# Four indirect row scatters of a GpSimd slot, moved from its end into two pairs between the norm and modulation steps

## What is computed

```python
h = layernorm(x) * (1 + ca) + sa          # norm 1 and its modulation
h = ln(h, ln1_g, ln1_b)                   # norm 2
xm = mix(h, att_time_mix, att_combined_mix)
k, v, r = exp(min(xm @ Wk.T, 60)), xm @ Wv.T, xm @ Wr.T
h = h + sigmoid(r) * wkv(time_decay, time_first, k, v) @ Wo.T
h = ln(h, ln2_g, ln2_b)                   # norm 3
xm = mix(h, ffn_time_mix, ffn_combined_mix)
h = h + sigmoid(xm @ Fr.T) * (square(relu(xm @ Fk.T)) @ Fv.T)
x = x + ga * h
h = layernorm(x) * (1 + cb) + sb          # norm 4 and its modulation
logits = h @ w_router.T                   # top 1 of 16 experts
x = x + gb * (shared_mlp(h) + sigmoid(top logit) * h through its expert)
```

## Time and profile before

| | before |
|---|---|
| median of 3 runs (lowest, highest) | 395.59 us (393.89, 396.46) |
| the profiled execution | 393.6 us |
| its span | 391.8 us |
| granted TensorE clock, mean | 0.858 of full |
| busy TensorE / VectorE / ScalarE / GpSimd | 296.8 / 244.0 / 179.3 / 187.6 us |
| GpSimd: the 32 scatters (L400) | 36.5 us busy, 1140 ns mean |
| GpSimd: the powers of the 32 rs steps (L377) | 33.2 us busy, 1038 ns mean |
| GpSimd idle ahead of rs (L375) | 59.5 us, 58.6 of it for VectorE's statistics (L432) |
| first scatter starts, last scatter starts | 95.3 us, 255.3 us |
| chain that ended last, by engine | PE 30%, DVE 24%, POOL 21%, issue 13%, ACT 7%, DMA 3% |

### The profile page before, as it was taken

One profiled execution on the slowest core, in us unless ns is written; L12 is line 12 of the kernel. 1 busy time (PEld: TensorE's weight loads), 2 busy tenths in 40 slices (PEclk: granted clock), 3 DMA queues, 4 the chain that ended last, 5 costly groups with the idle time before them and its releaser, 6 DMA issues.

```text
span 391.8 us, 4364 instructions
## 1 busy us (share of the span) xinstructions
PE 296.8 (76%) x1140; PEld 171.7 (44%) x1140; DVE 244.0 (62%) x514; ACT 179.3 (46%) x436; POOL 187.6 (48%) x267
## 2 busy tenths in 40 slices
PE   4363667877668766877795586699989999999844
PEld 4223234334433534544453343334436666666532
DVE  5148596997989889789688342634335444444423
ACT  2541654947556666555372543222214444444300
POOL 4542726558678485656273534310003666666610
PEclk9956598996998888767889598699999999999955
DMA  6688000102011010010010100132002222222057
GB/s 182 175 241 321 28 0 4 51 0 60 22 47 35 0 54 29 0 41 21 0 49 8 41 14 14 50 97 49 0 1 56 75 75 82 71 77 71 4 155 274
DMA packets 28184, 25.22 MB, mean 64 GB/s; under 512 B 3682, under 2 KB 21734, under 8 KB 28160
## 3 DMA queue, kind: packets, MB, share of 16 engines
q1 hardware_dynamic: 24480, 18.57, 16.5%
q0 software_dynamic: 2528, 4.27, 3.4%
q10 hardware_dynamic: 1152, 2.10, 1.4%
HBM read 17.42 MB, written 8.49 MB: 66 GB/s over the span
## 4 chain that ended last, share of the span: by engine, by line
PE 30%; DVE 24%; POOL 21%; issue 13%; ACT 7%; DMA 3%; SPq 0%; POOLq 0%; DVEq 0%; ACTq 0%
PE bank L858 23%; POOL y_rows L423 11%; PE bank L862 5%; DVE work L524 4%; POOL sorted_rows L400 4%; POOL work L377 3%; ACT work L724 2%; DMA work<-y_rows 2%; DVE work L543 2%; DVE work L519 2%; DVE work L517 1%; DVE work L541 1%; PE bank L901 1%; POOL work L381 1%; DVE work L528 1%
## 5 line engine op out<-in xcount | busy, mean ns | idle before, releaser
L423 POOL DMA_INDIRECT y_rows<-work x47 | 46.2, 982 | 71.2 <-ACT work L838 41.9
L862 PE MATMUL bank<-ident,work 128*128 128x128 f32 x192 | 40.2, 362 | 52.9 <-ACT work L724 23.9
L862 PEld LDWEIGHTS bank<-ident,work 128*128 128x128 f32 x192 | 29.9, 185 | 75.0 <-ACT work L724 28.9
L858 PE MATMUL bank<-up_experts,work 128*128 x94 | 48.2, 595 | 0.0
L685 DVE COPY work<-bank 128x256 f32<-128x256 f32 x47 | 19.9, 424 | 37.7 <-PE bank L1043 37.7
L400 POOL DMA_INDIRECT sorted_rows<-rows,slot_i x32 | 36.5, 1140 | 14.4 <-issue 8.9
L858 PE MATMUL bank<-work,Fk 128*128 128x512 f32 x64 | 34.9, 652 | 5.7 <-DVE work L506 5.7
L724 ACT ACTIVATE work<-work 128x128 f32<-128x128 f32 x64 | 26.3, 487 | 23.5 <-POOL work L381 23.5
L375 POOL TENSOR_SCALAR work<-work 128x4 f32<-128x4 f32 x32 | 6.7, 210 | 59.5 <-DVE work L432 58.6
L377 POOL TENSOR_TENSOR work<-work,neghalf 128x4 f32<-128x4 f32 x32 | 33.2, 1038 | 2.7
L858 PE MATMUL bank<-work,Fv 128*128 128x512 f32 x64 | 33.3, 648 | 0.0
(11 more groups left out here) (161 smaller groups left out, 630.4 us busy)
## 6 DMA issues: line engine op xcount, KB each, us to landing
up_experts<-in_gate_up SPq DMA_DIRECT2D x2, 2048.0 KB, 11.7
work<-sorted_rows SPq DMA_DIRECT2D x47, 66.0 KB, 1.8
work<-in_x SPq DMA_DIRECT2D x8, 256.0 KB, 3.4
work<-in_xT SPq DMA_DIRECT2D x8, 256.0 KB, 3.1
work<-y_rows SPq DMA_DIRECT2D x8, 256.0 KB, 4.2
out_t<-work ACTq DMA_DIRECT2D x8, 256.0 KB, 3.9
sorted_rows<-pad_row SPq DMA_DIRECT2D x17, 66.0 KB, 1.6
y_rows<-work POOLq DMA_INDIRECT x47
```

The costliest lines, as they stand in the source:

```text
L423: pool.indirect_dma_start(y_rows, bass.IndirectOffsetOnAxis(number[q], 0), yb[q], None, bounds_check=NB * T - 1, oob_is_err=False).then_in ...
L858: return pe.matmul(out, w, x, start=start, stop=stop)
L862: last = pe.transpose(out[:, j * P:(j + 1) * P], src[:, j * P:(j + 1) * P], ident[:])
```

## The change

`scatter` gets two arguments, the first tile and the number of tiles. In GpSimd's slot loop it is called twice, with two tiles each time: behind rs(0, s), ahead of rs(2, s-2), and behind modulate(s), ahead of rs(3, s-3). The call at the slot's end goes. Both calls keep the two waits of `scatter`. All other engines keep their instructions and their order.

```diff
-            def scatter(b):
+            def scatter(b, first, tiles):
                 pool.wait_ge(A_rows.sem, A_rows.after(b))
                 pool.wait_ge(B_slot.sem, B_slot.after(b))
-                for n in range(b * NT, (b + 1) * NT):
+                for n in range(b * NT + first, b * NT + first + tiles):
                     pool.indirect_dma_start(sorted_rows, bass.IndirectOffsetOnAxis(slot_i[:, n:n + 1], 0),
                                             rows[:, n, :], None).then_inc(B_out.sem, 16)
...
                 if batch(s):
                     rs(0, s)
+                if batch(s - 4):
+                    scatter(s - 4, 0, NT // 2)
                 if batch(s - 2):
                     rs(2, s - 2)
                 if batch(s):
                     modulate(s)
+                if batch(s - 4):
+                    scatter(s - 4, NT // 2, NT // 2)
                 if batch(s - 3):
                     rs(3, s - 3)
-                if batch(s - 4):
-                    scatter(s - 4)
```

## The result

The changed kernel takes 424.5 us, the median of 4 runs (422.13 to 426.65), against 395.22 us (393.89 to 396.46) for the kernel before: 1.074 times as long, 95% interval 1.067 to 1.081. The kernel before ran again beside each experiment, and its executions fall into two groups, 388 to 391 and 394 to 398 us (its profile is at 393.6), so ratios against it can differ by 1 to 2% where the kernels' own times don't. The forecast was 414 us with a range of 404 to 422. The direction was right, and so was the place of the second mix; the loss of 29 us is more than half as large again as the 18 forecast, and lies above the range.

A forecast was written before the change was run, and what follows sets the result against it. Slot 7 was read as bound by a chain with 6.0 us of scatters, slots 4 and 5 by VectorE's 16.0 us. Terms 11.0 + 4.3 + 3.8 + 1.0 = 20.1 us gave 414 us, range 404 to 422.

The forecast's parts named there:

- (a): Scatters leave the path between rs(3) and rs(1), or are cheap in their new place: faster, down to 370 us; 3 in 100.
- (b): No effect, 394 to 397 us: slot numbers come early and GpSimd's idle time ahead of rs(3) absorbs the pair; 5 in 100.
- the hole of slot 7: GpSimd's 3.4 us idle between the modulation's end and rs(3) in slot 7, which a pair would fit in length.
- Step 1: Earliest start of the first pair: the cast ending the slot numbers is over 2.25 us after the slot's first mix.
- Step 3: Slots 4 to 7: second mix 12.1 us after the first; with 16.0 us of VectorE work behind it, at least 28.1 us.
- Steps 5 and 6: Slots 8 and 9: a later second mix adds 4.3 us in slot 8 and 3.8 us in slot 9.
- the other line: Slots 4 to 7: path through second pair, rs(3), norm 4 rows, t4 and t1 to the next mix, 28.4 to 30.4 us.
- Step 4: Slots 4 to 7, path over rs(3) and t1: 29.0 us taken for each slot, +11.0 us together.
- rival (c): TensorE at 1.2 GHz adds up to 3 us a slot, about 426 us; 10 in 100 for above 422.
- VectorE's line: Slots 4 to 7: unbroken VectorE work from second mix to next first mix, 16.0 us, giving at least 28.1 us a slot.
- Step 7: Slot 10: four scatters ahead of rs(3) delay it, +1.0 us, or +2 with dear pairs; slot 11 unchanged.
- The low end: Sum of all low terms, 4.2 + 3.5 + 3.0 + 0.6 = 11.3 us, giving 405 us.

The follow-up runs named there:

- The ladder: Kernel before with one, two or three scatters moved ahead of rs(2), the rest at the slot's end: 402.8, 412.6 and 423.0 us.
- pe_filler: Changed kernel plus three useless matmuls ahead of TensorE's wait before t4 in slots 4 to 7: 415.9 us against 424.1.
- first_pair_only: Kernel before with only the first scatter pair moved ahead of rs(2), the second pair left at the slot's end: 412.6 us, ratio 1.059.
- before_filler: Kernel before plus three useless matmuls ahead of t1's wait from slot 4 on: 387.2 us, ratio 0.990 (0.977 to 1.003).

## Why the prediction missed its size

**Right.** Rivals (a) and (b) fell as argued: no pair was cheap enough to gain, and the hole of slot 7 took nothing in. Step 1 said slot numbers at M+2.25; they came at M+2.26. Step 3 said the second mix at M+12.1; it came at M+12.08, though three of its terms were off and cancelled: first issue 0.8 for 0.2, pair 2.9 (148.24 to 151.11) for 3.3, rs(2) 1.9 for 2.3. That it came out so close is luck. The ladder shows the step itself, 1.26 us for each scatter. Steps 5 and 6 gave +4.3 and +3.8 where +4.7 and +4.2 were measured. That the other line would be the longer one was right.

**Step 4 failed, in two terms.** It added up the other line with durations from the kernel before, where that work stood elsewhere.

- *From t4 to t1, 4.9 us.* It measured 7.4 in slot 6 (6.2 and 6.5 in slots 4 and 5, 7.5 in slot 7). The step took a stretch at 2.4 GHz from the earlier trace rows, while the same step made ScalarE, and so t4, wait for an rs(3) that is 6 us late. pe_filler shows that a filled wait gives 4.8. The prediction had this as rival (c), at 10 in 100, outside the forecast. It belonged in the sum: the earlier trace rows had eight transposes at 1.97 us behind a wait of 3.34 in slot 7, and at 1.09 behind a wait of 2.95 in slot 4.
- *rs(3), 2.3 us.* It measured 3.7 in each of the four slots (in slot 6 from 158.19 to 161.92), its small operations 0.68, 0.61 and 1.14 us instead of about 0.2 to 0.6. Three of them end with a VectorE operation: L375 at 158.87 and the second mix's L508 at 158.81, L379 at 160.70 and the scan at 160.67, L381 at 161.92 and the second scan at 161.93. The second pair pushed rs(3) from ahead of the second mix onto the scans. In first_pair_only, where only its last operation runs beside the second mix (155.37), rs(3) takes 2.4 us (153.78 to 156.19). This is read from traces; no run isolates it. The page "SBUF — State Buffer" of the Trainium skill, section "Who interferes with whom", says that a VectorE operation with two SBUF inputs and a GpSimd operation that reads SBUF hold one port pair in turn; the trace agrees: the 0.20 us of L375 become 0.68.

**Why the halves cost 7.2 us and the whole 15.2.** A slot takes the longer of two lines. With the second pair alone t4 already waits 3.3 us, t1 stands at M+22.3 (188.38 against 166.09) and gives the slot's 27.1 us. With the first pair alone t4 has no wait and VectorE's line gives 27.9 us. With both, the delay by the first pair falls on the line of the second: rs(3) ends at M+16.7 instead of M+12.9, t1 stands at M+25.8, and the slot takes 3.5 us more than with the second pair alone.

The line of step 4 from 28.4 us, with the terms as slot 6 measured them: the second pair over 1.2 us earlier (M+13.0 for M+14.2; the pairs took 2.9 and 2.4 us for 3.3 each), rs(3) 1.4 longer, t4 to t1 2.5 longer, t1 to the next mix 4.8 for 5.4. That is 28.4 - 1.2 + 1.4 + 2.5 - 0.6 = 30.5, and the slot took 30.55. The forecast took 29.0, and the four slots together measured 4.2 us more than it.

**Step 7** gave +1.0 and the two last parts measured +3.9. GpSimd's timeline in slot 10 (S = 258.37, where before S was 233.70):

```profile
259.84 1.53 POOL L400 DMA_INDIRECT sorted_rows<-rows,slot_i  x1 [3.80 <-DVE slot_i L587]
...
265.25 0.19 POOL L375 TENSOR_SCALAR work<-work 128x4 f32<-128x4 f32 x1
```

rs(3) starts at S+6.9 instead of S+4.9, so +2.0: 0.8 until the first issue and 5.4 us for four scatters, the dear end of the step. The other 1.9 us lie behind it and were not traced to a cause.

**The first issue** behind a wait was costed at 0.2 us, from a scatter behind other work, and measured 0.8. The kernel before had such a scatter, in slot 11; it was the nearer row:

```profile
251.50 0.95 POOL L400 DMA_INDIRECT sorted_rows<-rows,slot_i  x1 [5.58 <-DVE slot_i L585]
```

**The low end** of the sum has 3.0 and 0.6 us for steps 6 and 7, where the steps themselves give 3.4 and 1.0; it would be 406 us, and nothing hangs on it.

**What bounds the kernel** was incomplete. "6.0 us of scatters stand on the path in slot 7" is true of the chain, but before_filler shows that slots 6 and 7 were long because of 1.2 GHz behind t1's wait.

**In sum:** 4.2 for slots 4 to 7, 0.8 for slots 8 and 9, 2.9 for slot 10 and behind, and 0.6 ahead of the first scatter, which the change does not explain, are the 8.5 us between 20.1 and 28.6. Rival (c), which gave about 426, stood outside the range at 10 in 100; the measured 424.5 is near it.

## What to carry to other kernels

Where each engine works in a written order, price a moved step by what is queued behind its wait and its issue, followed through every other engine's queue as well; and look for its new place where the engine will still wait afterwards, for a batch whose inputs are long done. A hole read from one slot moves with the rhythm: work out where it lies after the change before filling it. If the change puts a wait ahead of matmuls, cost what follows at both clocks from the rows that have them, in the sum and not only as a rival. The length of the wait alone does not tell which it will be: in the kernel before t1 took 1.09 us behind a wait of 2.95 us in slot 4, and 1.97 us behind a shorter one in slot 7:

```profile
183.18 1.97 PE L862 MATMUL bank<-ident,work 128*128 128x128 f32 x8 [2.82 <-ACT work L724]
```

## What the hardware showed that was not expected

A scatter that GpSimd issues right behind a semaphore wait starts 0.8 us behind the releasing operation's end, where an ordinary operation starts 0.14 us behind it, and one behind other work 0.17 us. Behind the first of a group the next one starts 1.4 to 1.8 us later in the changed kernel, and each further one 1.26 us later; two cost 2.4 to 2.9 us and four 5.4. The power of 128x4 values takes 1.04 us alone and up to 1.55 us beside VectorE's WKV operations (162.70 in the changed kernel). Three matmuls that compute nothing, put into a wait of TensorE in each of four slots, took 8 us out of 424.
